# Where the join between attention and routed experts is reordered: bias products, scatters, first weights, and two moves inside the image loop

## The reference

```python
h = tok_ref(x, w, b)                                  # 14 x 14 patches of 16 x 16: (32, 196, 128)
h = concatenate([h, txt], axis=1)                     # 273 tokens
h = h + attn_ref(layernorm(h), w_qkv, b_qkv, w_pre, w_post, w_out, b_out)
h = h + ffn_ref(layernorm(h), Wg, W1, b1, W2, b2, ln_g, ln_b, out_g, out_b)

# attn_ref: 8 heads of 16, rotary positions
logits = einsum('bhid,bhjd->bhij', q, k) * scale
logits = einsum('bhij,gh->bgij', logits, w_pre)             # heads mixed before the softmax
attn = einsum('bhij,gh->bgij', softmax(logits), w_post)     # and after it
out = einsum('bhij,bhjd->bhid', attn, v) @ w_out.T + b_out

# ffn_ref: 8 experts, the best two of each token
xn = layer_norm(x, ln_g, ln_b)
top_p, top_i = top_k(softmax(xn @ Wg), 2)
conf = top_p / top_p.sum()
o_e = gelu(xn @ W1[e] + b1[e]) @ W2[e] + b2[e]              # 128 -> 512 -> 128
return layer_norm(x + sum_k conf_k * o_{top_i[k]}, out_g, out_b)
```

## Time and profile before

| | |
|---|---|
| median of 3 runs | 1492.24 us (1491.61 to 1493.64) |
| the profiled execution | 1497.27 us, of which its span 1495.4 us |
| busy share of the span | PE 83%, PEld 71%, DVE 63%, ACT 68%, POOL 57% |
| images (first part) | until about 1066 us |
| join, until the first tile is transposed | 1066 to 1083 us |
| tiles (second part) | 1083 to 1364 us |
| third part | 1364 us to the end |

### The profile page before, as it was taken

One profiled execution on the slowest core, in us unless ns is written; L12 is line 12 of the kernel. 1 busy time (PEld: TensorE's weight loads), 2 busy tenths in 40 slices (PEclk: granted clock), 3 DMA queues, 4 the chain that ended last, 5 costly groups with the idle time before them and its releaser, 6 DMA issues.

```text
span 1495.4 us, 34349 instructions
## 1 busy us (share of the span) xinstructions
PE 1242.3 (83%) x8194; PEld 1064.1 (71%) x8195; DVE 949.0 (63%) x3348; ACT 1021.6 (68%) x3007; POOL 852.1 (57%) x1653
## 2 busy tenths in 40 slices
PE   5899999999999999999999999998199999995000
PEld 4677777777777777777777777777099999994000
DVE  4776667767677676677666776663245454444887
ACT  2687878778777878787787877874055555553665
POOL 2135545555555655556555555553546666665998
PEclk9999999999999999999999999997589999998555
DMA  5001110101101011010111010100222222221554
GB/s 227 18 27 39 48 31 30 34 30 51 34 30 34 30 49 36 30 34 30 39 42 34 30 34 30 35 18 17 61 68 76 76 79 74 77 78 54 156 158 128
DMA packets 69455, 82.29 MB, mean 55 GB/s; under 512 B 11626, under 2 KB 59725, under 8 KB 68898
## 3 DMA queue, kind: packets, MB, share of 16 engines
q1 hardware_dynamic: 57216, 57.16, 13.2%
q0 software_dynamic: 11328, 19.07, 4.1%
q10 hardware_dynamic: 866, 5.55, 0.9%
HBM read 52.08 MB, written 30.65 MB: 55 GB/s over the span
## 4 chain that ended last, share of the span: by engine, by line
PE 41%; POOL 21%; issue 18%; DVE 12%; ACT 4%; POOLq 1%; DMA 1%; DVEq 1%; SPq 1%; ACTq 0%
PE PS L1411 9%; PE PS L1174 6%; PE PS L1258 5%; PE PS L1220 4%; PE PS L1398 3%; PE PS L1399 2%; PE PS L1400 2%; POOL rs L626 2%; DVE nmax L923 2%; POOL nr L507 2%; DVE VP L890 2%; POOL cf L525 2%; DVE bst L845 2%; POOL EK L495 2%; DVE sl L982 2%
## 5 line engine op out<-in xcount | busy, mean ns | idle before, releaser
L1220 PE MATMUL PS<-kT,qs 128*128 128x273 f32 x1024 | 280.1, 396 | 2.2 <-ACT E L668 1.8
L1258 PE MATMUL PS<-AT,VP 128*128 128x273 f32 x1024 | 278.4, 394 | 0.0
L923 DVE TENSOR_REDUCE nmax<-PS 128x2 f32<-128x546 f32 (+1 forms) x288 | 206.1, 715 | 73.1 <-PE PS L1220 73.1
L668 ACT ACTIVATE E<-PS,nmax 128x273 f32<-128x273 f32 x512 | 243.4, 483 | 11.8 <-DVE nmax L923 9.1
L556 POOL DMA_INDIRECT dram_routed<-xr,slu x192 | 189.5, 987 | 64.8 <-issue 64.8
L1220 PEld LDWEIGHTS PS<-kT,qs 128*128 128x128 f32 x1024 | 184.1, 190 | 36.1 <-issue 2.9
L607 POOL DMA_INDIRECT dram_results<-arena,du x152 | 166.3, 1094 | 64.2 <-issue 54.6
L695 ACT COPY AT<-PS 128x512 f32<-128x512 f32 x256 | 151.0, 590 | 67.8 <-PE PS L1238 65.5
L1258 PEld LDWEIGHTS PS<-AT,VP 128*128 128x128 f32 x1024 | 175.0, 191 | 20.4
L1238 PEld LDWEIGHTS PS<-small,E 128*128 128x128 f32 x1024 | 125.7, 140 | 46.8 <-ACT ATR L702 16.3
L1238 PE MATMUL PS<-small,E 128*128 128x128 f32 x1024 | 155.8, 274 | 3.0 <-ACT ATR L702 0.6
(11 more groups left out here) (187 smaller groups left out, 2745.5 us busy)
## 6 DMA issues: line engine op xcount, KB each, us to landing
arena<-in_x SPq DMA_DIRECT2D x32, 588.0 KB, 3.8
arena<-dram_routed SPq DMA_DIRECT2D x76, 144.0 KB
stage<-dram_results SPq DMA_DIRECT2D x32, 196.0 KB
dram_h<-H SPq DMA_DIRECT2D x32, 147.0 KB
w1hl<-dram_h SPq DMA_DIRECT2D x32, 147.0 KB
out<-w1hl SPq DMA_DIRECT2D x32, 98.0 KB
dram_routed<-xr,slu POOLq DMA_INDIRECT x192, 2.3
stage<-dram_results SPq DMA_DIRECT2D x32, 77.0 KB
```

The lines of the kernel that those rows point to most:

```text
L668: nc.scalar.activation(bank, PS[0:rows, 2 * ((par + u) % 2) + t, 0:N], ACT.Exp, bias=nmax[0:rows, u, t:t + 1], accum_out=esum[0:rows, u, t ...
L923: v.tensor_reduce(nmax[0:rows, u], PS[0:rows, b0:b0 + 2, 0:N], AX.X, ALU.max, negate=True).then_inc(S["max"], 1)
L1220: last = mm(PS[0:rows, 2 * ((par + u) % 2) + t, 0:N], q, kT[:, par, 0:N], start=True, stop=True)
L1258: last = mm(acc, VP[:, par, g, c, :], AT[:, g, c, :], start=(g == 0 and c == 0), stop=False)
```

## The change

Seven edits, at four places.

1. TensorE computes the bias products (`shifted_bias`) behind all steps and no longer in turn 4 of step 32, and waits there until `b1f` is written. VectorE adds `b1` behind the table. The table's two work arrays move from `stage`, which holds the weights for these products, to `AT`.
2. In step 33 GpSimd issues the first three scatters of image 30 in turn 0 and the other three behind the masks, in turn 8; before, all six stood ahead of the masks.
3. VectorE copies the weights of the first two tiles ahead of the tile stages; ScalarE evaluates gelu once on one column behind the steps.
4. Inside the loop ScalarE copies the attention sums at the start of turn 3, and the transposed probabilities of this turn behind the scaling; TensorE transposes for the gate behind the first half of the patch products.

```diff
-        cmp_, cda = (stage[0:1, i, 0:TILES * NE].rearrange("p (n e) -> p n e", e=NE) for i in range(2))
+        cmp_, cda = (AT[0:1, 2 * i:2 * i + 2].rearrange("p h c n -> p (h c n)")[:, 0:TILES * NE].rearrange(
+            "p (n e) -> p n e", e=NE) for i in range(2))
...
-                    if u == (0 if has["res"] else 7) and has["late"]:
+                    if u == 0 and has["late"]:
                         scatter(i - 3, 1 - par, 0)
-                    if u == (1 if has["res"] else 7) and has["late"]:
+                    if u == 1 and has["late"] and has["res"]:
                         scatter(i - 3, 1 - par, 1)
...
+                    if u == 8 and has["late"] and not has["res"]:
+                        scatter(i - 3, 1 - par, 1)
...
                     head = behind(i, u, 3, has)
-                    if head:
+                    if u == 3 and has["res"]:
+                        attn_out(i - 1)
+                    if head and u != 3:
                         probsT(*head)
...
                         q_hi(lead[0], par if u + 3 < NU else 1 - par, lead[1] - 1)
+                    if head and u == 3:
+                        probsT(*head)
...
-                    if u == 3 and has["res"]:
-                        attn_out(i - 1)
...
+            nc.scalar.activation(warm[:], lng[:, 0:1], ACT.Gelu_apprx_tanh)
             act.wait_ge(S["b1_kept"], 1)
...
-            dve.wait_ge(S["b1_ps"], 1)
-            v.tensor_tensor(b1f[:], PS[:, 0, 0:NE * FC], b1c[:], ALU.add).then_inc(S["b1_kept"], 1)
-
...
+            dve.wait_ge(S["b1_ps"], 1)
+            v.tensor_tensor(b1f[:], PS[:, 0, 0:NE * FC], b1c[:], ALU.add).then_inc(S["b1_kept"], 1)
+
...
+            for first in range(2):
+                weights(first, first, dve.value_load(tab[0:1, 0, first:first + 1], min_val=0, max_val=NE - 1))
+
+            def later_weights(t, u, e):
+                if not below(t, 2):
+                    weights(t, u, e)
...
-            slots(dve, TILES, [(2, split), (2, weights), (1, columns), (0, result)], (weights, columns))
+            slots(dve, TILES, [(2, split), (2, later_weights), (1, columns), (0, result)], (later_weights, columns))
...
-                    if u == 4 and not has["attn"] and has["res"]:
-                        shifted_bias()
...
-                    if u == 1 and has["rout"]:
-                        x2T_(i - 2, par)
                     if u == 2 and has["rout"]:
                         gate(i - 2)
...
                             qk(i + 1, u - 6, 1)
+                    if u == 1 and has["rout"]:
+                        x2T_(i - 2, par)
...
             steps(pe, step)
+            shifted_bias()
+            pe.wait_ge(S["b1_kept"], 1)
```

More of the change, by code:

```diff
@@ L211, in early_fusion_kernel @@
         XB = arena[:, 0:UP * TH * ROW].rearrange("p (u h c) -> p u h c", u=UP, h=TH)
+        warm = sb("warm", [128, 1])
         b1f = sb("b1f", [128, NE * FC])
```

## The result

The changed kernel takes 1480.49 us in the median of 4 runs (1477.81 to 1481.11), against 1492.14 (1491.61 to 1493.64) of the kernel before: a ratio of 0.9917, 95% interval 0.99 to 0.9934. That is 11.65 us faster (9.8 to 14.9 by the interval); the prediction had 15.65. The profiled execution of the changed kernel took 1477.81 us, of which 1476.0 are its span.

A forecast was written before the change was run, and what follows sets the result against it. The prediction took a ring through the engines to bound the images, with everything in line at the join. Its terms summed to -15.65 us, from 1497.3 to 1481.6 profiled, so 1476.6 for the median; range 1469 to 1484.

The forecast's parts named there:

- a ring: Image loop: value rows, patch products, scores, maxima, then VectorE and GpSimd up to the next value rows set the time.
- TensorE's sum of work: Rival for the loop: TensorE's total work is the bound, so both loop waits are pure gain; 1418 us, chance 0.03.
- Gating shifted, +7.0: Loop: gate transposes moved behind the first patch products cost their 0.25 us slot in each of 28 images.
- Attention sums, -1.4 and -1.1: Loop: copying the sums earlier gains 0.05 us in 28 images (1.4), and one projection wait in the last attention step (1.1).
- Bias products, -12.2: Join: the last projection starts without waiting for the bias products and runs at full clock; 12.2 us less.
- Scatters, -6.7: Join: splitting image 30's scatters around the last masks brings the first tile load 6.7 us earlier (5.5 to 6.9).
- First weights, -1.25: First tile: the first hidden product no longer waits for VectorE's weight copy; 1.25 us less, bounds 0 and 1.25.
- Gelu, nothing: Join: the early gelu table load gains nothing, since the first tiles' half clock covers the old load.
- the hole fully closed: Loop, bound of the attention sums: VectorE's 0.17 us wait for the exponentials vanishes in 28 images, 4.8 us.
- The sign of being wrong that came closest: Join: the prediction is wrong if the first tile comes less than 17 us earlier against the last image.
- Full clock in the first tiles: Rival: the first tiles run at the full clock, saving 1.8 us more; 1474.8 us, chance 0.06.
- lost clock in the loop: Rival: longer TensorE gaps ahead of the patch products lower the clock there, 44 us more; 1520 us, chance 0.05.

The follow-up runs named there:

- e8: Changed kernel with the gate transposes back in the gap ahead of the patch products and issued twice; 1470.98 us, one run.
- e9: Changed kernel with the gate transposes, left behind the first patch products, issued twice; 1488.18 us, one run.
- e13: Changed kernel with only VectorE's copy of the gate logits moved to the start of turn 3; 1479.28 us, one run.
- e11: Changed kernel with VectorE's places behind the value rows and GpSimd's second scatter moved behind its norm; 1450.89 us, 0.9726 of before.
- e1: Changed kernel with the gate transposes back in the gap ahead of the patch products; 1472.01 us, 0.9862 of before.
- e2: Changed kernel with the attention sums copied behind the exponentials again; 1481.83 us, 0.9931 of before.
- e4: Kernel before with only the bias products moved behind the ranks, with the bias sum and work arrays this needs; 1480.58 us, 0.9926.
- e12: e11 with VectorE's copy of the gate logits also moved to the start of turn 3; 1449.37 us, 0.9715 of before.
- e5: Kernel before with only image 30's scatters split around the masks; 1482.89 us, 0.9949 of before.
- e3: Kernel before with only the two moves inside the loop (attention sums and gate transposes); 1497.9 us, 1.0042 of before.
- e6: Changed kernel without the early copy of the first two tiles' weights; 1482.14 us, one run.
- e7: Changed kernel without the early gelu on one column; 1479.60 us, one run.

## Why the prediction was right, and where its sizes were off

*What bounds the loop.* Right: a ring, and not TensorE's sum of work (e8, e9, e13). Its hand-overs between VectorE and GpSimd, which the prediction left as one piece, have a place: VectorE's wait for `tokb` ahead of the value rows. The trace of the kernel before shows this wait already, and the prediction did not read it:

```profile
DVE pos L978 <- POOL tokb L546: 75.4, 31, 10.5
```

Putting `places` with its wait behind the value rows (e11, together with the later scatter) is worth 29.6 us, more than all seven edits.

*Gating shifted, +7.0.* Right mechanism, a little larger: 0.28 an image (changed against e1), 0.32 with the sums in their old place (e2 against e4: 824.96 - 816.64 over 26 images). The slot is 0.26, and the scores behind the transposes are 0.94 from the next start (500.56 to 501.50) where in the kernel e1 they are 0.92, which makes the 0.28. What the rest of the 0.32 is stays open.

*Attention sums, -1.4 and -1.1.* The step that failed is the sentence that TensorE's wait at the projection would be gone and that the query and key products would be late next. The projection also waits for the copy of the logits out of the same PSUM bank, which VectorE makes behind the statistics; the prediction did not read that second condition. Some 0.8 of the wait stayed where it was. The price hardly changed, as the ring has it: 0.05 an image with the gating shifted (e2 against the changed kernel), 0.01 without (e1 against e4), which is within what these stretches vary. When e12 and e13 took the logits away, the wait went where the prediction had put it, but not for its reason: not the normalised rows are late there but ScalarE's copy of their transposes. The last step gave hardly half of its 1.1: 0.43 for the last three images and that step together.

*Bias products, -12.2.* Confirmed in kind: the projection directly behind the sums, at the upper clock. In size 11.2, since the products took 12.32 us in the profile of before, with the clock falling among them, and 11.03 and 11.41 in e5 and e3, which have them in the same place. That is a term sized from one execution.

*Scatters, -6.7:* 6.3 and 6.5. In the changed kernel the last scatter decided and no longer the tail rows: the wait of SyncE is put down to the scatters (first row below), and the last of them starts at 1062.67 and lands 2.70 later (second row, from the chain of waits). The prediction had the two nearly level.

```profile
SPq L388 <- DMA dram_routed<-xr,slu: 2.8, 1, 2.8
```

```profile
1062.67 2.70 DMA dram_routed<-xr,slu
```

*First weights, -1.25:* 1.4 (3.03 to 1.64, and e6). *Gelu, nothing:* e7 agrees: the first gelu with its table load ends at 1073.39 + 1.57 = 1074.96, before the second product at 1075.30. That the half clock is this cover, as the prediction said, is argued: no run has the first tiles at the full clock.

*The sum again, from measured terms:* both loop moves with the last step (823.70 + 80.55) - (816.64 + 80.65) = +7.0, bias -11.2, scatters -6.4, weights -1.4: -12.0, against -11.65 in the medians. Of the 3.9 us that the forecast was too low, 2.5 lie in the loop with the last step (+4.5 forecast), 1.0 in the bias products and 0.3 in the scatters, and the first weights gave some 0.15 more than forecast; the rest, some 0.2, is far inside the interval of the medians, so it proves nothing of the single terms. The range's lower end needs a correction: with the hole fully closed 4.8 stands in place of the 1.4, so by the prediction's own terms it is 1473.2 and not 1471.

*The sign of being wrong that came closest:* the first tile should come at least 17 us earlier. Counted from the projection of image 28 it takes 114.91 us, 18.9 less than in the profile of before (133.82) and 17.6 less than in e3 (132.51), which has the same loop.

*Full clock in the first tiles, lost clock in the loop:* neither. The first tile starts at 0.50, and the 13.79 us of unbroken one-column products ahead of it ran at 0.50 throughout. The Trainium skill, page "TensorE: Matmul & The Clock Gate", Part 1, has activity release the half clock; for these products the trace does not agree. In the loop gaps of 1.08 and 1.49 us in turn left the clock at 1.00 from 120 to 1030 us. The same Part 1 of the Trainium skill's page "TensorE: Matmul & The Clock Gate" has idle time bring the half clock back; no run here shows that for gaps as short as these.

The fastest kernel of the study is e12, 0.9715 of before; e11 without the logits is within its uncertainty. Neither was run with the gate transposes back in the gap: by the code these wait until the places have read their bank, and the late places stand behind the value rows, so TensorE would wait there. The changed kernel itself is not the best form of its own edits: with the gating move taken back (e1) it is 8.5 us faster.

## What to carry to other kernels

Before a wait is taken away, list every condition of the waiting instruction, not only the one that the profile names, since the next one stands there as soon as the first is gone. Follow the ring by what ends last on each engine, and look in it for an instruction that waits for another engine while nothing behind it needs its result: putting it behind the work that others wait for was worth more here than everything at the join (29.6 us against 19.0). Test whether a gap has room by doing the small work in it twice.

## What was not expected of the hardware

The same 64 instructions of the bias products took 13.79 us at 0.50 throughout, and 12.32, 11.41 and 11.03 (before, e3 and e5) where the clock fell among them. So the fall of the clock on the critical path made the time there not only longer but different from execution to execution, by 1.3 us in these three. The part behind the tiles (from TensorE's last instruction to the end), with the same code in all, took 126.9 us in e5 and 130.8 in the profile of before; what makes it vary was not looked into.
